# Attention on one Trainium2 core: value products of two steps together, maxima over two adjoining PSUM banks, first group's maxima in the projection stage

## The chip, the cores and the metric

The kernel is one program on one core of a Trainium2 chip. The metric is the device time of one execution in microseconds (us). The engines are called as in the profile: PE (TensorE matmuls), PEld (its weight loads), DVE (VectorE), ACT (ScalarE), POOL (GpSimd), SP (SyncE, which here only issues DMAs). PSUM has eight banks of 512 fp32 columns.

## The reference

One layer of a mixed model, on x of shape 4 x 1024 x 256 (4096 tokens): low-rank multi-head attention, a spiking feed-forward block, a selective scan (Mamba-like), and the feed-forward block again, each with a norm and a residual. The change touches attention only:

```
xn = layernorm(x)                        # per token, 256 channels
q  = latent_q @ Wu_q + rope(latent_q @ Wq_r)
k  = latent_kv @ Wu_k + rope(xn @ Wk_r)
v  = latent_kv @ Wu_v                    # 16 heads of 16 channels
p  = softmax(q @ k.T / sqrt(272))        # 1024 x 1024 per head and batch
x  = x + (p @ v) @ Wo + bo
```

## The kernel before

`program` calls `project`, `attend`, `merge_heads`, `feed_forward`, `scan` and `feed_forward` in turn; each is a block of its own with a program for every engine, joined by semaphores. Engines take their instructions strictly in the order in which they are written.

**project** runs over 8 tiles of 512 tokens (two per batch). PE computes latents, rotary and compact parts in fp32. DVE joins them (`rotate`, `join`); ACT and POOL split each result into three bf16 parts (`high`, `middle`, `lower_parts`); SP stores the parts to the DRAM scratch `qk_parts`, 16 DMAs a tile (L216). `parts` has one buffer, so `high` of a tile waits for the stores of the tile before (`parts_out`). At tile 6 SP also loads the stacks of group 0 with `load_stack` (13 DMAs, L532 and L535).

**attend** works on 16 groups; a group is 4 heads of one batch. The bf16 parts are stacked along the contraction (96 rows), so that one bf16 matmul gives scores of near fp32 accuracy; three more rows carry the negated row maxima, which are subtracted in the same matmul. Three kinds of matmul are interleaved on PE:

- `for_max` (L762): scores with queries on the partitions, for the *next* group. 64 units of 128 x 512, in three PSUM banks by turns (`max_bank`, `MB` = 3). DVE's `maximum` (L864) reduces each to one column. Each `for_max` waits on `reduced` until the unit three before it has been reduced.
- `scores` (L776): scores with keys on the partitions, for the current group, in two pairs a step. Each pair fills a two-bank tile `score_bank[pair]` (4 banks in all), and ACT takes its exp (L852) into `probs`, which has two buffers, one a step.
- `pv` (L819): 4 matmuls of 32 output rows each, one for each head, side by side in the array; fp32, so each makes two passes and the trace shows eight records. They accumulate in `o_bank` (one bank) over 8 steps, one half group. `keep_o` (DVE, L883) then copies it out and SP stores it.

A group has 16 steps, and a step of PE is: scores pair 0, M0, scores pair 1, M1, M2, `pv` of the step before, M3, where M0 to M3 are four `for_max` units. Twice a group `turn` (PE, L769) transposes the row maxima of a half and `negate` (DVE, L877) negates them; POOL splits them in three (`split`) and SP writes them in as stack rows. `groups` runs 15 groups as 5 passes of a hardware loop, three groups a pass; at the end of a pass PE drains (`pv` of step 15). The 16th group comes behind it, without `for_max`.

The maxima of group 0 have no group before them. They stand ahead of the loop in `attend`: PE makes 32 pairs of matmuls into the two score tiles (L831), DVE reduces each pair, 1024 wide, straight into `row_max` (L912).

Of the kernel before, what the change touches and what calls it, by code (L numbers as in the profile page):

```python
# [118 lines left out]
def project(nc, io, xT, vT, split_scr, q_stack, k_stack):  # L119
# [6 lines left out]
    with ExitStack() as ctx:  # L126
        m = Mem(nc, ctx)
        ident = m.sb("ident", [P, P])
# [24 lines left out]
        comp_bank = [m.bank(f"comp_bank{c}") for c in range(DC)]  # L153
        rot_bank = [m.bank(f"rot_bank{c}") for c in range(DC)]
# [10 lines left out]
        stack_in = m.sem("first_stack_in")  # L165
# [15 lines left out]
        OUT = 16 * NG  # L181
        block = ctx.enter_context(nc.Block())
# [6 lines left out]
        def _(sp):  # L189
# [12 lines left out]
            for t in range(NT):  # L202
# [16 lines left out]
            sp.wait_ge(stack_in, STACK_LOAD)  # L219
            for u in range(CHUNKS):  # L220
                sp.wait_ge(parts_out[u], OUT * NT)

        @block.gpsimd
        def _(pool):
            nc.gpsimd.memset(mean_w[:], 1.0 / D).then_inc(consts_set, 1)
            nc.gpsimd.memset(eps_col[:], EPS).then_inc(consts_set, 1)

# [29 lines left out]
            lower_parts(NT - 1, 0)  # L257

        @block.tensor
        def _(pe):  # L260
# [45 lines left out]
            def rotary(t, side):  # L306
                for c in range(DC):
                    cols = slice(c * P, (c + 1) * P)
                    if side == 1:
# [3 lines left out]
                        for k in range(DC):  # L313
                            mm = nc.tensor.matmul(rot_bank[c][:], wkr[:, k, cols], xn[:, t % 2, k],
                                                  start=(k == 0), stop=(k == DC - 1))
                    else:
# [3 lines left out]
                        mm = nc.tensor.matmul(rot_bank[c][:], wq[:, 1, cols], ct[:, 0], start=True, stop=True)  # L320
                    mm.then_inc(proj_ready, 1)

            def compact(t, side):
                for c in range(DC):
# [4 lines left out]
                    mm = nc.tensor.matmul(comp_bank[c][:], wkc[:, cols] if side == 1 else wq[:, 0, cols], ct[:, side],  # L329
# [23 lines left out]
            for t in range(NT):  # L353
# [12 lines left out]
                if t + 2 < NT:  # L366
                    mean(t + 2)

# [70 lines left out]
        def _(dve):  # L439
# [26 lines left out]
            def rotate(t, side):  # L466
# [7 lines left out]
                for c, tables in enumerate(((cos, sin), (sin, cos))):  # L474
                    dve.wait_ge(proj_ready, t * UNITS + (ROT_K if side == 1 else ROT_Q) + c + 1)
                    for i, table in enumerate(tables):
                        nc.vector.scalar_tensor_tensor(r[:, 2 * c + i], rot_bank[c][:], bias[:, c:c + 1], table,
                                                       ALU.add, ALU.mult).then_inc(rotated, 1)

            def join(t, side):  # L480
# [3 lines left out]
                for c in range(DC):  # L484
# [3 lines left out]
                    nc.vector.scalar_tensor_tensor(comp_bank[c][:], comp_bank[c][:], bias[:, c:c + 1], r[:, 3 * c],  # L488
                                                   ALU.add, ALU.add).then_inc(rotated, 1)
                for c in range(DC):  # L490
# [6 lines left out]
                    nc.vector.tensor_tensor(full[:, u], comp_bank[c][:], r[:, 2 - c], ALU.subtract if c == 0 else ALU.add)\  # L497
# [15 lines left out]
            for t in range(NT):  # L513
# [8 lines left out]
                join(t, 0)  # L522

# [48 lines left out]
def attend(nc, io, vT, split_scr, q_stack, k_stack, o_scr, recip_scr, early, done_with):  # L572
# [10 lines left out]
    MB = 3  # L583
    TURN_NOW, TURN_NEXT = 2, 10
    with ExitStack() as ctx:
        m = Mem(nc, ctx)
        qs = [q_stack] + [m.sb(f"qs{i}", [P, 2, G, TW], BF16) for i in (1, 2)]
        ks = [k_stack] + [m.sb(f"ks{i}", [P, G, S], BF16) for i in (1, 2)]
        vg = [m.sb(f"vg{i}", [P, QT, G, 2 * HD]) for i in range(3)]
        ident = m.sb("ident_a", [P, P])  # L590
        probs = m.sb("probs", [P, 2, G, TW])
        mx = m.sb("mx", [P, 2, HU])
        row_max = m.sb("row_max", [P, 2, HU // 2])
        neg_max = m.sb("neg_max", [HU // 2, 2, P])
        neg_rest = m.sb("neg_rest", [HU // 2, 2, P])
        neg_parts = m.sb("neg_parts", [HU // 2, 2, 3, P], BF16)
# [4 lines left out]
        max_bank = [m.bank(f"max_bank{i}") for i in range(MB)]  # L601
# [3 lines left out]
        ident_in, ones_set, v_set = m.sem("ident_in"), m.sem("ones_set"), m.sem("v_set")  # L605
# [30 lines left out]
        def _(sp):  # L636
            sp.sem_clear(done_with)
            for h in range(2):
                sp.sem_inc(max_rows_in[h], 16)
# [48 lines left out]
            sp.dma_start(ident[:], io["ident"]).then_inc(ident_in, 16)  # L688

            sp.sem_inc(stack_in[0], STACK_LOAD)  # L690
            load(1, 1)
            max_rows(0, 0, 0)
# [12 lines left out]
        def _(pool):  # L705
            pool.sem_inc(neg_split, 8)
            for i in range(3):
                nc.gpsimd.memset(ks[i][SROWS:MROWS], 1.0).then_inc(ones_set, 1)

                pool.wait_ge(ones_set, 2 * i + 1)  # L710
                nc.gpsimd.memset(vg[i][:, :, :, HD:], 1.0).then_inc(ones_set, 1)
                pool.wait_ge(ones_set, 2 * i + 2)
# [32 lines left out]
            pool.wait_ge(ones_set, 6)  # L745
            v_of(0, 0)
            split(0, 0)
# [5 lines left out]
        def _(pe):  # L753
            pe.sem_inc(scores_ready, 1)
            pe.sem_inc(pv_done, 3 * STEPS)

            def for_max(g, r, a):
# [4 lines left out]
                nc.tensor.matmul(max_bank[(r + a) % MB][:], qs[r][0:SROWS, half, j, qt * P:(qt + 1) * P],  # L762
# [17 lines left out]
            def body(g, r, it, with_next):  # L780
                for s in range(STEPS):
                    if s % QT == 0:

                        pe.wait_ge(max_rows_in[s // QT], g * 48 + 64)
                    if s == 0 and with_next:
# [21 lines left out]
                if r == 2 or not with_next:  # L807
                    pv(g, r, STEPS - 1)

            def pv(g, r, s):  # L810
                qh, kt = s // QT, s % QT
                if s == 0:
                    pe.wait_ge(v_set, g + 1)
                if kt == 0:
# [3 lines left out]
                for j in range(G):  # L818
                    mm = nc.tensor.matmul(o_bank[32 * j:32 * j + 32, :], vg[r][:, kt, j], probs[:, s % 2, j],  # L819
# [3 lines left out]

            pe.wait_ge(stack_in[0], STACK_LOAD)
# [1275 lines left out]
```

## Time and profile before

| | us |
|---|---|
| median of 3 runs | 2124.3 (2123.36 to 2128.74) |
| the profiled execution | 2120.39 |
| its span, first to last instruction | 2118.6 |
| project | 0 to about 179 |
| attend, maxima of group 0 | about 180 to 220 |
| attend, 15 looped groups | 220.6 to about 930 |
| attend, last group | about 930 to 966 |
| merge, feed-forward, scan, feed-forward | the rest |

Mean granted TensorE clock: 0.954 of full speed. A timeline row gives start and length in us, engine, line, output and inputs, a count of merged instructions, and in brackets how long the engine stood idle before and what ended that. In merged rows the length goes from the first start to the last end; records of neighbouring matmuls overlap, since PE is pipelined.

### The profile page before, as it was taken

To read this page: it belongs to the slowest core of one execution; us is meant where nothing else is said; L and a number is where in the kernel's file an instruction comes from. 1 tells how busy PE (TensorE), PEld (TensorE's weight loads), DVE (VectorE), ACT (ScalarE), POOL (GpSimd) and SP (SyncE) were. 2 spreads that over 40 slices of the span, in tenths; PEclk is the share of its full clock that TensorE was granted. 3 is DMA by queue.
4 is the path that set the end of the run, shared out by engine and by line. 5 is a ranking of instruction groups with operands and counts; after the bars stand their busy time and mean duration, and the time that the engine had idled before them with its cause. 6 is when DMAs were issued, how large, how long until landed. Compare 5 with 4: busy or idle time off the path is not lost. (4 is left out here: it accounts for less than half of the span.)

```text
span 2118.6 us, 25344 instructions
## 1 busy us (share of the span) xinstructions
PE 1935.5 (91%) x6834; PEld 728.5 (34%) x6834; DVE 1673.7 (79%) x2442; ACT 1063.5 (50%) x1400; POOL 754.8 (36%) x518
## 2 busy tenths in 40 slices
PE   8996999999999999998999988788878888799997
PEld 4441232322232323323444433333333333234443
DVE  5887898998998989964565568999999999955554
ACT  3441566666666666672222236576567657422221
POOL 2664000000000000000100028999999999810000
PEclk9996899999999999999999999899999999999999
DMA  3454122231221222213100004444544445300000
GB/s 105 113 120 85 36 41 47 49 61 44 41 46 42 41 47 41 41 51 115 40 0 0 0 15 126 121 116 115 121 112 118 118 117 155 90 0 20 15 15 30
DMA packets 94683, 138.30 MB, mean 65 GB/s; under 512 B 13616, under 2 KB 52800, under 8 KB 93024
## 3 DMA queue, kind: packets, MB, share of 16 engines
q1 hardware_dynamic: 94560, 136.79, 26.8%
q8 instruction: 61, 1.00, 0.2%
q14 instruction: 62, 0.51, 0.1%
HBM read 110.27 MB, written 26.08 MB: 64 GB/s over the span
## 5 line engine op out<-in xcount | busy, mean ns | idle before, releaser
L864 DVE TENSOR_REDUCE mx<-max_bank 128x1 f32<-128x512 f32 x960 | 617.9, 687 | 57.9 <-PE max_bank L762 57.5
L852 ACT ACTIVATE probs<-score_bank 128x1024 f32<-128x1024 f32 x512 | 496.6, 1021 | 295.0 <-PE score_bank L776 294.7
L762 PE MATMUL max_bank<-ks,qs 96*128 96x512 bf16 x960 | 333.4, 388 | 0.0
L776 PE MATMUL score_bank<-qs,ks 99*128 99x512 bf16 x1024 | 310.5, 386 | 15.0 <-issue 13.2
L1538 POOL TENSOR_TENSOR ring<-u,bc 128x1024 f32<-128x1024 f32 x128 | 301.6, 2364 | 10.0 <-ACT u L1734 10.0
L1608 PE MATMUL ys_bank<-outs,rec_diag 128*128 128x512 f32 x512 | 254.1, 627 | 43.5 <-POOL outs L1546 22.0
L819 PE MATMUL o_bank<-probs,vg 128*32 128x512 f32 x2048 | 272.7, 605 | 0.7 <-ACT probs L852 0.7
L1546 POOL TENSOR_TENSOR outs<-ring,bc 128x1024 f32<-128x1024 f32 x109 | 257.7, 2364 | 25.6 <-DVE ring L1941 25.6
L728 POOL CAST neg_parts<-neg_max 16x128 bf16<-16x128 f32 x32 | 9.0, 281 | 682.8 <-DVE neg_max L877 682.8
L1783 ACT ACTIVATE a_bank<-dt,decay_s 128x512 f32<-128x512 f32 x256 | 169.5, 684 | 146.8 <-DVE ring L1941 103.5
L1332 ACT ACTIVATE relu_f<-hid_bank_f 128x512 f32<-128x512 f32 x128 | 76.4, 597 | 327.5 <-PE hid_bank_f L1285 282.4
L1357 DVE SCALAR_TENSOR_TENSOR hid_f<-hid_bank_f,relu_f 128x512 f32<-128x512 f32 x128 | 86.9, 688 | 189.5 <-ACT relu_f L1332 188.5
L1261 PE MATMUL y_bank_f<-hid_f,wpr_f 128*128 128x512 f32 x512 | 234.2, 592 | 0.5 <-DVE hid_f L1357 0.5
L1932 DVE SCALAR_TENSOR_TENSOR ring<-a_bank,ring 128x512 f32<-128x512 f32 x256 | 171.5, 670 | 24.3 <-ACT a_bank L1783 23.9
L762 PEld LDWEIGHTS max_bank<-ks,qs 96*128 96x128 bf16 x960 | 93.7, 98 | 277.9 <-DVE mx L864 184.2
L1608 PEld LDWEIGHTS ys_bank<-outs,rec_diag 128*128 128x128 f32 x512 | 100.9, 201 | 184.7 <-issue 134.8
L982 POOL TENSOR_TENSOR sq_sum_f<-sq_f 128x512 f32<-128x512 f32 x16 | 20.2, 1265 | 390.1 <-ACT sq_f L1009 390.1
L776 PEld LDWEIGHTS score_bank<-qs,ks 99*128 99x128 bf16 x1024 | 99.0, 99 | 121.7 <-issue 25.2
L1261 PEld LDWEIGHTS y_bank_f<-hid_f,wpr_f 128*128 128x128 f32 x512 | 95.9, 190 | 120.7 <-issue 115.8
L1941 DVE TENSOR_TENSOR_SCAN ring<-a_bank,ring 128x512 f32<-128x512 f32 x112 | 135.6, 1211 | 0.0
L1941 DVE TENSOR_TENSOR_SCAN ring<-a_bank,state,ring 128x512 f32<-128x512 f32 x106 | 134.8, 1271 | 0.0
L1285 PE MATMUL hid_bank_f<-xn_f,wfc_f 128*128 (+1 forms) x256 | 119.5, 600 | 3.2 <-POOL eps_col_f L951 3.2
(198 smaller groups left out, 2150.6 us busy)
## 6 DMA issues: line engine op xcount, KB each, us to landing
bc<-bc_scr SPq DMA_DIRECT2D x128, 512.0 KB, 4.9
qk_parts<-parts SPq DMA_DIRECT2D x128, 96.0 KB, 1.9
qs<-qk_parts SPq DMA_DIRECT2D x128, 64.0 KB, 4.3
o_scr<-o_sb SPq DMA_DIRECT2D x32, 256.0 KB, 2.1
ks<-qk_parts SPq DMA_DIRECT2D x16, 384.0 KB, 4.7
xin<-in_x_dram SPq DMA_DIRECT2D x8, 512.0 KB, 3.9
ks<-qk_parts SPq DMA_DIRECT2D x16, 256.0 KB, 3.5
qs<-qk_parts SPq DMA_DIRECT2D x32, 128.0 KB, 4.8
```

The costliest lines, as they stand in the source:

```text
L762: nc.tensor.matmul(max_bank[(r + a) % MB][:], qs[r][0:SROWS, half, j, qt * P:(qt + 1) * P], ks[r][0:SROWS, j, kh * TW:(kh + 1) * TW], star ...
L776: mm = nc.tensor.matmul(score_bank[pair][:, j % 2], ks[r][0:MROWS, j, kt * P:(kt + 1) * P], qs[r][0:MROWS, qh, j, :], start=True, stop=True)
L819: mm = nc.tensor.matmul(o_bank[32 * j:32 * j + 32, :], vg[r][:, kt, j], probs[:, s % 2, j], start=(kt == 0), stop=(kt == QT - 1))
L852: nc.scalar.activation(probs[:, s % 2, 2 * pair:2 * pair + 2], score_bank[pair][:], ACT.Exp, scale=SOFTMAX_SCALE).then_inc(probs_ready, 1)
L864: nc.vector.tensor_reduce(mx[:, a // HU, a % HU:a % HU + 1], max_bank[(r + a) % MB][:], AX_X, ALU.max)\
L1261: mm = nc.tensor.matmul(y_bank[c][:], wpr[:, f, c * P:(c + 1) * P], hid[:, f], start=(f == 0), stop=(f == FC - 1))
L1538: nc.gpsimd.tensor_tensor(ring[:, g % RING], u[:, t % 2], bc[:, g % BC, 0:1].to_broadcast([P, DC, TW]), ALU.mult).then_inc(inputs, 1)
L1546: nc.gpsimd.tensor_tensor(outs[:, g % OUTS], ring[:, g % RING], bc[:, g % BC, 1:2].to_broadcast([P, DC, TW]), ALU.mult).then_inc(weighted, 1)
L1608: mm = nc.tensor.matmul(y_bank[f][:], rec_diag[:, f * NS + n], outs[:, g % OUTS, f], start=(n == 0), stop=(n == NS - 1))
L1783: nc.scalar.activation(a_bank[g % 2][:, f], dt[:, t % 2, f], ACT.Exp, scale=a_col[:, f, n:n + 1])\
L1932: nc.vector.scalar_tensor_tensor(x, a, 1.0, x, ALU.subtract, ALU.mult).then_inc(scaled, 1)
L1941: nc.vector.tensor_tensor_scan(a if on_dve(g) else x, a, x, state[:, f, n:n + 1] if t % TPB else 0.0, ALU.mult, ALU.add)\
```

## The change

Four edits, all in the attention part:

1. **Value products together.** `pv` runs on even steps only and then for the two steps before. `probs` gets four buffers (`KEPT`). `keep_o` goes from DVE to ACT and stands behind the exps of steps 0 and 8.
2. **Maxima over two banks.** The three max banks become one tile `max_banks`. Where a unit lies in bank 0, `maximum` takes it and the next one (bank 1) in one instruction of 2 x 512; units in bank 2 are taken alone. It waits for both matmuls, and raises `reduced` by two when it is done.
3. **First group.** The 32 wide maxima of group 0, the turn, negation, splitting and writing of their first half go to the end of `project`'s programs, in the banks of rotary and compact parts. The stacks of groups 0 and 1 are both loaded by SP at tile 3 (before: group 0 at tile 6, group 1 at the start of `attend`).
4. **Constants.** POOL sets the ones rows of two stacks at the start of `project`, and the other ones behind the first `v_of` in `attend`; PE waits for them at its first `pv` and at step 8. The identity is shared, its second load is gone.

```diff
 def project(...)
+        max_banks = (rot_banks, comp_banks)
 @sync
-                if t == NT - TPB:
+                if t == TPB + 1:
                     for u in range(CHUNKS):
-                        sp.wait_ge(parts_out[u], OUT * t)
-                    load_stack(sp, split_scr, q_stack, k_stack, 0, stack_in)
+                        sp.wait_ge(parts_out[u], OUT * TPB)
+                    for g in range(2):
+                        load_stack(sp, split_scr, begun[f"qs{g}"], begun[f"ks{g}"], g, stack_in)
...
+            sp.wait_ge(neg_split, 4)
+            for part in range(3):
+                sp.dma_start(begun["qs0"][SROWS + part:SROWS + part + 1, 0], neg_parts[:, 0, part, :]).then_inc(neg_in, 16)
 @gpsimd
+            for g in range(2):
+                nc.gpsimd.memset(begun[f"ks{g}"][SROWS:MROWS], 1.0).then_inc(ones_set, 1)
+                pool.wait_ge(ones_set, g + 1)
 @tensor, behind the last tile
+            pe.wait_ge(stack_in, 2 * STACK_LOAD)
+            for n in range(PAIRS):
+                if n == 0:
+                    pe.wait_ge(rotated, (NT - 1) * SIDES * ROTS + ROTS + 4)
+                elif n == 1:
+                    pe.wait_ge(summed, NT * CHUNKS)
+                else:
+                    pe.wait_ge(unit_max, n - 1)
+                for kh in range(2):
+                    mm = nc.tensor.matmul(max_banks[n % 2][:, kh], ...)
+                mm.then_inc(unit_ready, 1)
 @vector, behind the last tile
+            for n in range(PAIRS):
+                dve.wait_ge(unit_ready, n + 1)
+                nc.vector.tensor_reduce(row_max[:, half, i:i + 1], max_banks[n % 2][:].rearrange("p a t -> p (a t)"),
+                                        AX_X, ALU.max).then_inc(unit_max, 1)

 def attend(...)
+    KEPT = 4
-        probs = m.sb("probs", [P, 2, G, TW])
+        probs = m.sb("probs", [P, KEPT, G, TW])
+        max_banks = ctx.enter_context(nc.psum_tensor("max_banks", [P, MB, TW], F32))
+        max_bank = [max_banks[:, i] for i in range(MB)]
 @gpsimd
+            nc.gpsimd.memset(vg[0][:, :, :, HD:], 1.0).then_inc(ones_set, 1)
...
+            v_of(0, 0)
+            for i in (1, 2):
+                nc.gpsimd.memset(vg[i][:, :, :, HD:], 1.0).then_inc(ones_set, 1)
+            nc.gpsimd.memset(ks[2][SROWS:MROWS], 1.0).then_inc(ones_set, 1)
 @tensor
-                    if s > 0:
-                        pv(g, r, s - 1)
-                    elif r > 0:
-                        pv(g - 1, r - 1, STEPS - 1)
+                    if s % 2 == 0:
+                        if s > 0:
+                            pv(g, r, s - 2)
+                            pv(g, r, s - 1)
+                        elif r > 0:
+                            pv(g - 1, r - 1, STEPS - 2)
+                            pv(g - 1, r - 1, STEPS - 1)
 @scalar
-                    act.wait_ge(pv_done, g * STEPS + (3 * STEPS + s - 1))
+                    act.wait_ge(pv_done, g * STEPS + (3 * STEPS + s - KEPT + 1))
...
+                    if s == 0 and r > 0:
+                        keep_o(g - 1, 1)
+                    if s == QT:
+                        keep_o(g, 0)
 @vector
             def maximum(g, r, a):
-                dve.wait_ge(max_ready, g * UNITS + a + 1)
-                nc.vector.tensor_reduce(mx[:, a // HU, a % HU:a % HU + 1], max_bank[(r + a) % MB][:], AX_X, ALU.max)\
-                    .then_inc(reduced, 1)
+                bank = (r + a) % MB
+                if bank == 1 and a:
+                    return
+                n = 2 if bank == 0 and a + 1 < UNITS else 1
+                dve.wait_ge(max_ready, g * UNITS + a + n)
+                nc.vector.tensor_reduce(mx[:, a:a + n], max_banks[:, bank:bank + n], AX_X, ALU.max).then_inc(reduced, n)
-            def keep_o(g, qh):
-                nc.vector.tensor_copy(o_sb[:, qh], o_bank[:]).then_inc(o_kept, 1)
```

## Rows read from the trace of the kernel before

**Rows 1.** The page: busy time, share of the span, instructions.
```profile
PE 1935.5 (91%) x6834; PEld 728.5 (34%) x6834; DVE 1673.7 (79%) x2442; ACT 1063.5 (50%) x1400; POOL 754.8 (36%) x518
```

**Rows 2.** Timeline of PE in the loop: start, length in us, line, tiles, idle before.
```profile
442.65 0.39 PE L762 MATMUL max_bank<-ks,qs 96*128 96x512 bf16 x1
...
443.97 0.60 PE L762 MATMUL max_bank<-ks,qs 96*128 96x512 bf16 x2
444.49 1.07 PE L819 MATMUL o_bank<-probs,vg 128*32 128x512 f32 x8
445.49 0.39 PE L762 MATMUL max_bank<-ks,qs 96*128 96x512 bf16 x1
```

**Rows 3.** The same stretch on DVE, then on ACT.
```profile
443.08 2.59 DVE L864 TENSOR_REDUCE mx<-max_bank 128x1 f32<-128x512 f32 x4 [0.25 <-PE max_bank L762]
...
443.51 1.94 ACT L852 ACTIVATE probs<-score_bank 128x1024 f32<-128x1024 f32 x2 [0.96 <-PE score_bank L776]
```

**Rows 4.** Timeline of DVE: two negations of neighbouring halves.
```profile
299.39 0.28 DVE L877 TENSOR_SCALAR neg_max<-max_bank 16x128 f32<-16x128 f32 x1 [0.23 <-PE max_bank L769]
...
322.31 0.28 DVE L877 TENSOR_SCALAR neg_max<-max_bank 16x128 f32<-16x128 f32 x1 [0.22 <-PE max_bank L769]
```

**Rows 5.** Waits from 250 to 900 us (in total, times, longest); then line 819.
```profile
PEld max_bank L762 <- DVE mx L864: 168.7, 218, 0.8
...
L819 PE MATMUL o_bank<-probs,vg x2048: 589/593/618, 226.4 to 965.1; 128*32 128x512 f32 x187
```

**Rows 6.** Timeline of all engines, first step of a loop pass.
```profile
364.16 4.33 DVE L864 TENSOR_REDUCE mx<-max_bank 128x1 f32<-128x512 f32 x7 [2.86 <-PE max_bank L762]
...
364.91 0.10 PEld L762 LDWEIGHTS max_bank<-ks,qs 96*128 96x128 bf16 x1 [0.41 <-DVE mx L864]
```

**Rows 7.** Groups by line: the wide maxima; then timeline of PE, fp32 matmuls.
```profile
L912 DVE TENSOR_REDUCE row_max<-score_bank 128x1 f32<-128x1024 f32 x32 | 37.7, 1220 | 12.2 <-PE score_bank L831 11.2 <-DVE row_max L912 0.2
...
118.87 1.88 PE L303 MATMUL lat_bank<-xn,wdq 128*128 128x512 f32 x4
```

**Rows 8.** Timeline of the last group.
```profile
958.43 3.90 ACT L852 ACTIVATE probs<-score_bank 128x1024 f32<-128x1024 f32 x4 [0.32 <-PE score_bank L776]
...
964.66 1.07 PE L819 MATMUL o_bank<-probs,vg 128*32 128x512 f32 x8 [0.66 <-ACT probs L852]
```

**Rows 9.** Timeline between projection and the loop.
```profile
155.86 21.31 SPq L216 DMA_DIRECT2D qk_parts<-parts  x32
...
168.68 1.28 DVE L497 TENSOR_TENSOR full<-comp_bank,rot 128x512 f32<-128x512 f32 x2
...
179.98 1.89 PE L831 MATMUL score_bank<-ks,qs 96*128 96x512 bf16 x4 [13.72 <-SPq L690]
...
181.13 19.32 DVE L912 TENSOR_REDUCE row_max<-score_bank 128x1 f32<-128x1024 f32 x16 [11.17 <-PE score_bank L831]
...
220.57 1.03 PE L776 MATMUL score_bank<-qs,ks 99*128 99x512 bf16 x2 [1.89 <-issue]
```

**Rows 10.** Projection: the queue of SP, then ACT.
```profile
98.44 11.04 SPq L216 DMA_DIRECT2D qk_parts<-parts  x16
...
148.03 1.27 SPq L532 DMA_DIRECT2D ks<-qk_parts  x3
149.34 6.48 SPq L535 DMA_DIRECT2D qs<-qk_parts  x10
...
110.58 1.15 ACT L408 ACTIVATE parts<-full 128x512 bf16<-128x512 f32 x2
...
...
117.41 0.67 ACT L400 ACTIVATE ct<-lat_bank,bcol 128x512 f32<-128x512 f32 x1
```

**Rows 11.** Windows: stretch, length, busy time by engine (instructions), granted clock, DMA.
```profile
190.00:205.00 15.00, 12.82 (x27) 1.71 (x25) 14.48 (x13) 0.00 (x0) 2.16 (x3) 0.50 0.01 2
646.00:652.00 6.00, 5.99 (x15) 2.09 (x15) 3.27 (x5) 3.30 (x4) 0.00 (x0) 0.50 0.02 4
950.00:960.00 10.00, 9.75 (x60) 1.81 (x58) 0.10 (x1) 9.29 (x10) 0.39 (x1) 1.00 0.52 160
```

More of the change, by code:

```diff
@@ L152, in project @@
         norm_bank, lat_bank = m.bank("norm_bank"), m.bank("lat_bank")
-        comp_bank = [m.bank(f"comp_bank{c}") for c in range(DC)]
-        rot_bank = [m.bank(f"rot_bank{c}") for c in range(DC)]
+        comp_banks, rot_banks = (ctx.enter_context(nc.psum_tensor(n, [P, DC, TW], F32)) for n in ("comp_banks", "rot_banks"))
+        comp_bank, rot_bank = ([banks[:, c] for c in range(DC)] for banks in (comp_banks, rot_banks))
         ident_in, consts_in = m.sem("ident_in"), m.sem("consts_in")
@@ L600, in attend @@
         recip_parts = m.sb("early_parts", [2 * EARLY, 3, TW], BF16)
-        max_bank = [m.bank(f"max_bank{i}") for i in range(MB)]
+        max_banks = ctx.enter_context(nc.psum_tensor("max_banks", [P, MB, TW], F32))
+        max_bank = [max_banks[:, i] for i in range(MB)]
         score_bank = [m.ctx.enter_context(nc.psum_tensor(f"score_bank{i}", [P, 2, TW], F32)) for i in range(2)]
         o_bank = m.bank("o_bank")
-        ident_in, ones_set, v_set = m.sem("ident_in"), m.sem("ones_set"), m.sem("v_set")
+        ones_set, v_set = m.sem("ones_set"), m.sem("v_set")
         stack_in = [m.sem(f"stack_in{i}") for i in range(3)]
@@ L686, in body @@
                 o_to_dram(g, 1)
[L688 to L692, printed above, removed]
+            for g in range(2):
+                sp.sem_inc(stack_in[g], STACK_LOAD)
             with sp.Fori(0, (NGT - 4) // 3) as it:
@@ L705, in _ @@
         def _(pool):
[L706 to L712, printed above, removed]
+            pool.sem_inc(neg_split, 12)
+            nc.gpsimd.memset(vg[0][:, :, :, HD:], 1.0).then_inc(ones_set, 1)
+            pool.wait_ge(ones_set, 1)
             def v_of(g, r):
@@ L761, in for_max @@
                 pe.wait_ge(reduced, g * UNITS + a + 1)
-                nc.tensor.matmul(max_bank[(r + a) % MB][:], qs[r][0:SROWS, half, j, qt * P:(qt + 1) * P],
+                nc.tensor.matmul(max_bank[(r + a) % MB], qs[r][0:SROWS, half, j, qt * P:(qt + 1) * P],
                                  ks[r][0:SROWS, j, kh * TW:(kh + 1) * TW], start=True, stop=True)\
@@ L813, in pv @@
                     pe.wait_ge(v_set, g + 1)
+                    pe.wait_ge(ones_set, 3)
                 if kt == 0:
@@ L818, in pv @@
                 for j in range(G):
[L819 removed]
+                    mm = nc.tensor.matmul(o_bank[32 * j:32 * j + 32, :], vg[r][:, kt, j], probs[:, s % KEPT, j],
                                           start=(kt == 0), stop=(kt == QT - 1))
                 mm.then_inc(pv_done, 1)
[L824 to L839 removed]
+            pe.wait_ge(ones_set, 1)
             groups(pe, body)
@@ L891, in body @@
                             negate(g + 1, 0, turn_bank(r, s))
-                        if i == 3 and s == 0 and r > 0:
-                            keep_o(g - 1, 1)
-                        if i == 3 and s == QT:
-                            keep_o(g, 0)
                         if with_next:
@@ L904, in body @@
                     both_halves(g + 1, 1)
-                if r == 2 or not with_next:
-                    keep_o(g, 1)
-            for n in range(HU):
-                half, i = n // (HU // 2), n % (HU // 2)
-                dve.wait_ge(max_ready, 2 * n + 2)
-                nc.vector.tensor_reduce(row_max[:, half, i:i + 1], score_bank[n % 2][:].rearrange("p a t -> p (a t)"),
-                                        AX_X, ALU.max).then_inc(reduced, 2)
-                if i == HU // 2 - 1:
-                    dve.wait_ge(reduced, 2 * n + 2 + MB)
-                    nc.vector.sem_inc(row_max_ready, 1)
-                if n == HU // 2 + 3:
-                    negate(0, 0, max_bank[0])
             groups(dve, body)
```

127 lines of the change are left out of this document (79 added, 48 removed).

## The prediction

> **What bounds the kernel now.** I read the page's busy shares first, then the main loop of attend between 250 and 900 us in the waits and the timelines of PE, DVE and ACT, then the two ends of attend. Over the whole span PE is busy for 91% and DVE for 79% [rows 1], but a busy PE is not yet a bound, so the loop itself has to be read. There are 15 groups with a next group (five loop passes of three) and a last one without. A step of such a group is, on PE, score pair, M0, score pair, M1, M2, the value product (PV) of the step before, M3; M0 to M3 are the matmuls of `for_max`. [rows 2] show it in steady state. From 442.65 (M3) to 443.97 (M1) six bf16 matmuls start in 1.32 us, 0.22 each. The second of the two at 443.97 would be through at 444.41; PV starts at 444.49, 0.08 later; its eight records take 1.00 until M3 starts at 445.49. So 8 x 0.22 + 0.08 + 1.00 = 2.84 us, the distance of the two M3: PE has no hole. DVE [rows 3] takes four maxima in 2.59 and then waits 0.25 for the M3 behind PV; ACT waits 0.96 in a step. PE bounds the loop, with DVE only 9% below it. The two negations at 299.39 and 322.31 [rows 4] are a whole half group apart: 22.92 = 8 x 2.84 + 0.20 for the transpose.
>
> The waits say that PE's weight loads stand 168.7 us for DVE's maxima [rows 5]. This is not lost time: loads wait while PV still streams. Where PV is absent it is real. In step 0 of a loop pass [rows 6] the maximum of M0, the first of seven, begins at 364.16 and ends 0.69 later, at 364.85; the load of M3, which needs that bank, starts at 364.91, its matmul 0.01 later. So a freed bank reaches PE after 0.07. The other way, M3 at 442.65 to its maximum at 443.08 is 0.43.
>
> **The change, part by part.**
>
> *Maxima over two adjoining banks.* A 1024 wide maximum lasts 1.220 [rows 7]; back to back 16 take 19.32 [rows 9], spaced (19.32 - 1.22)/15 = 1.21, against 2 x 0.63 for two narrow ones ([rows 3], (2.59 - 0.69)/3). That saves 0.05 of DVE time per pair, on an engine that isn't the bound. The Trainium skill (Perfetto Trace Analysis, Optimizing Scalar/DVE Operations) says grouping helps a saturated engine, since each access to PSUM costs DVE about 125 ns; but where DVE is unsaturated and holds up others, smaller instructions may finish sooner. By its 125 ns some 320 pairs would save 40 us of DVE time, by the rows 16; neither is PE time, and its second half speaks against the edit.
>
> The price is in the waits. `maximum` on bank 0 now waits for two matmuls, and both banks come free together. With three banks, call them b0, b1, b2. The next M on b0 must wait for the whole pair maximum, the one on b1 comes after it in PE's order, and only then can the next pair maximum start. From one pair maximum to the next: 1.22 (it lasts) + 0.07 + gap from M(b0) to M(b1) on PE + 0.43. Gaps: 0.22 where they adjoin, 0.66 with two score matmuls between, and with both PVs between 0.22 + 1.94 = 2.16 (1.94 below). 24 maxima, three double steps, have 8 such cycles, and bank 0 falls once on each of the 8 positions of a double step. The gaps then sum to PE's own time of one double step: 16 x 0.22 + 1.94 = 5.44. So 8 x 1.72 + 5.44 = 19.2. Two cycles are longer, as the two PVs stand between M(b1) and the next M(b0) and PE arrives late: with PVs behind M(b1) 2.16 + 0.66 - 0.43 - 1.29 = 1.10, behind M(b2) 0.22 + 2.16 - 0.43 - 1.29 = 0.66. Sum 20.96, or 6.99 per double step, against 2 x 2.84 = 5.68. That is +1.31, x 8 x 15 = **+157 us**. The maxima on b2 fit between the pairs (1.21 + 0.6 = 1.8, the shortest cycle is 1.94), so DVE isn't full: it waits. The new stall is PE's at `for_max`, with the scores and PVs behind it, and ACT behind them.
>
> *Value products of two steps together.* PE leaves and enters PV half as often. An fp32 pass of 512 columns takes (1.88 - 0.59)/3 = 0.43 [rows 7], 0.59 being one record of PV [rows 5]; a PV makes two passes on each of four column strips side by side, 0.86, so 1.00 + 0.08 holds 0.22 of entering and leaving. No row has two PVs adjoining. Bounds: two together cost 1.08 + 0.86 = 1.94 if this is paid once, 2.16 if it is paid each time. I take 1.94, since all eight records are the same form and the 0.22 stands at changes of form. The other end adds 0.22 x 120 = 26 us to the loop. Steps without PV let PE run into the maxima earlier; that is in the cycles above.
>
> *Four probability buffers.* Needed for the above; ACT's wait for `pv_done` lies two steps further back. No cost.
>
> *keep_o to ACT.* A 0.69 copy leaves DVE. On ACT it waits for the joined PV; it starts 0.1 behind it and takes some 0.6 (estimated from exps twice as wide, 1.0), while the next score pair needs 0.22 + 0.22 + 0.4 = 0.85. It hides in ACT's idle time (0.96 a step [rows 3]); uncovered it would be 32 x 0.6 = 19 us. I take 0.
>
> *Last group.* It has no maxima and is bound by the exp chain [rows 8]: four exps in 3.90 and 0.32 of waiting are two steps, 4.22. After two PVs ACT has run dry: score pair 0.63, two exps of 0.92, next score pair from 2.63, first PV at 3.15, plus 1.94, 5.1. Eight times 0.88: 7.0, less the 0.7 that the last PV waited: **+6 us**.
>
> *First group's maxima in projection.* Now DVE ends its last projection work at 169.96 and idles until 181.13; the 32 wide maxima then run to about 220 and the loop starts at 220.57 [rows 9]. They are DVE-bound, 1.21 each, and stay so. In the new place they begin at 170.0, as the banks come free, and hide the splitting and the stores that attend waited for: -11.2. But the switch of blocks now comes behind them. It costs the 0.9 us that PE needed before (SP's last store was issued by 177.17 and took the page's 1.9 to land, at 179.1; PE started at 179.98), the `ones_set` wait for one memset, 0.6, and perhaps cold loop code: +1.5 (0 to 3.5). On SP, 26 loads move to t = 3, where 13 stood at t = 6. Thirteen took 1.27 + 6.48 us to issue [rows 10], so 15.5 from about 91.7 to 107.3; the 16 stores that started at 98.44 start 8.9 late. `high` of the next tile (110.58) waits for their first eight, landed about 114.8 instead of 106; its second half for the last, landed about 120.2. ACT's latent copy at 117.41 is behind it and the PE tile behind that (118.87): about +2.7 (0 to 5), as PE has other matmuls until then. The loads at t = 6 go, without gain: the tile there was no longer than the rest. Two memsets of 3.5 us on POOL fall before its first work at 18.5. Sum: -11.2 + 1.5 + 2.7 = **-7 us**. The loads of groups 0 and 1 and the negated rows are there long before use; the constants set later (`ones_set` 3 and 4) are needed at step 2 and step 8, after 5 and 25 us, and take about 6 us of POOL.
>
> Total: the profiled execution took 2120.4 (span 2118.6). 2120.4 + 157 + 6 - 7 = 2276. The median of the three runs is 3.9 above the profiled one, so I forecast **2280** as a median.
>
> **Rivals.**
>
> *A, forecast, 0.84:* the coupled cycle sets the loop. Its own range is 2254 (handovers shorter by 0.07 in each of 320 cycles, -22; start part at its best, -4) to 2310 (PV saving nothing, +26; start part at its worst, +4).
>
> *B, faster, 0.06:* the pair never ends last and PE stays the bound. Then a double step is 5.44 + two PV margins, 5.46: 0.22 less, x 120 = -26; with -7 and +6 that is 2093 as a profiled execution, 2097 as a median. It decides at 8x + 5.44 + 1.76 = 17.04, x = 1.23 for maximum plus both handovers; the rows give 1.72. Against it: every term of 1.72 was read singly. For it: DVE loses 0.05 per pair and a copy per half group. The Trainium skill (TensorEngine Tiling (Array Packing), Key Properties) holds that changing the tiling mode drains the engine; the 0.22 of [rows 2] agrees with that.
>
> *C, between, 0.03:* the edges cancel, within 0.3% of 2124 (about what a measurement can tell from no change). It needs cycles of 1.3.
>
> *D, clock, 0.07:* with more holes PE falls to the 1.2 GHz level (granted 0.50) and stays. It stood at 0.50 from 190 to 205 in DVE-bound maxima [rows 11], yet at 1.00 in the last group with holes of 0.2 to 0.7; after the hole at a loop end it was 0.50 for some us of dense work, then full again. In the new loop PE has work for 5.4 of 7.0 us, its holes are under 1 us, and at half clock the work (some 10.5) would be dense again, after which it rose before. If one pass of five stayed low, 24 x (10.5 - 7.0) = 84 more: 2360; all of them, 2700.
>
> **Chances.** Faster 0.06, same 0.03, slower 0.91 (A and D). The range 2245 to 2315 is A's with 5 to 9 us beyond the ends for what isn't listed; B, C and D, 0.16 together, are left out, and some 0.04 of A.
>
> **What would show it.** Right: distances of score steps by pairs near 7.0 us; DVE's waits for `max_bank` near 1.1 us a step instead of 0.25; PE idle for maxima in the middle of steps; wide maxima 1.22; copies of `o_bank` on ACT right behind the second PV; the loop starting near 213.5 us; group distance 56 instead of 45.8. Two adjoining PVs in 1.94 or 2.16 settles that term. Wrong: a double step of 5.5, or a granted clock below 0.9 in the loop; or PE reaching M(b0) late so seldom that a cycle is 6.4.

## The result, and the profile after

The changed kernel takes **2298.8 us** (median of 4 runs, 2296.9 to 2301.9) against 2123.8 (2120.7 to 2128.7, 4 runs) for the kernel before: **1.082 times as long**, 95% interval 1.080 to 1.084. Slower was forecast, with 2280 and a range of 2245 to 2315. The profiled execution has a span of 2300.1 and a mean granted clock of 0.952 (before: 2118.6 and 0.954).

The page of the changed kernel: engine totals, then the granted clock in 40 slices, then three groups by line (idle time and its releaser behind the bar).

```profile
PE 1964.1 (85%) x6834; PEld 748.0 (33%) x6834; DVE 1627.8 (71%) x2095; ACT 1087.7 (47%) x1432; POOL 754.8 (33%) x518
...
PEclk9996999999999999999999999899999999899999
...
L937 DVE TENSOR_REDUCE mx<-max_banks 128x1 f32<-128x512 f32 (+1 forms) x645 | 589.0, 947 | 278.0 <-PE max_banks L826 277.8
L913 ACT ACTIVATE probs<-score_bank 128x1024 f32<-128x1024 f32 x512 | 501.3, 1022 | 393.0 <-PE score_bank L840 390.1
L826 PE MATMUL max_banks<-ks,qs 96*128 96x512 bf16 x960 | 338.9, 391 | 158.2 <-DVE mx L937 146.0
```

All three engines of attention have a lower share than in [rows 1], though PE's work is the same 6834 instructions: they wait for each other. The waits between 250 and 1100 us (in total, times, longest) say for whom:

```profile
ACT probs L913 <- PE score_bank L840: 332.3, 248, 4.3
PEld max_banks L826 <- DVE mx L937: 325.6, 323, 1.7
DVE mx L937 <- PE max_banks L826: 265.7, 336, 4.1
PE max_banks L826 <- DVE mx L937: 139.1, 210, 1.2
...
ACT o_sb L905 <- PE o_bank L890: 51.0, 28, 3.6
```

PE waits for DVE and DVE waits for PE, on the same line of each. In [rows 5] only the loads stood there, covered by PV; now PE's matmuls themselves do, 210 times. The coupled cycle can be seen one wait at a time. PE of the changed kernel (start, length, idle before):

```profile
451.17 0.38 PE L826 MATMUL max_banks<-ks,qs 96*128 96x512 bf16 x1
451.39 0.60 PE L840 MATMUL score_bank<-qs,ks 99*128 99x512 bf16 x2
451.82 0.59 PE L826 MATMUL max_banks<-ks,qs 96*128 96x512 bf16 x2
453.59 0.39 PE L826 MATMUL max_banks<-ks,qs 96*128 96x512 bf16 x1 [1.17 <-DVE mx L937]
453.82 0.60 PE L840 MATMUL score_bank<-qs,ks 99*128 99x512 bf16 x2
454.25 0.38 PE L826 MATMUL max_banks<-ks,qs 96*128 96x512 bf16 x1
```

and DVE beside it:

```profile
452.31 1.82 DVE L937 TENSOR_REDUCE mx<-max_banks 128x2 f32<-128x1024 f32 x2 [0.68 <-PE max_banks L826]
454.74 1.82 DVE L937 TENSOR_REDUCE mx<-max_banks 128x2 f32<-128x1024 f32 x2 [0.61 <-PE max_banks L826]
```

M(b0) stands at 451.17, but the wide maximum begins only at 452.31, behind M(b1) at 451.82. It lasts 1.22 (the row also holds the single maximum behind it) and so holds both banks until 453.53; M(b0) follows at 453.59, M(b1) at 454.25 (two score matmuls between them), and the next wide maximum starts at 454.74: 2.43 us from one to the next. This closed chain of waits, in which each engine waits for the other once a pair, is called the ring below.

### The profile page after: what moved, and what is told of

It reads as the page before. It is cut to its first block and busy times, and to the rows that moved or that the text cites. A ratio compares the mean times of both kernels' runs of the same rounds, so it can differ in the third digit from the quotient of the medians.

```text
span 2300.1 us, 25020 instructions
## 1 busy us (share of the span) xinstructions
PE 1964.1 (85%) x6834; PEld 748.0 (33%) x6834; DVE 1627.8 (71%) x2095; ACT 1087.7 (47%) x1432; POOL 754.8 (33%) x518
## 5 line engine op out<-in xcount | busy, mean ns | idle before, releaser
L937 DVE TENSOR_REDUCE mx<-max_banks 128x1 f32<-128x512 f32 (+1 forms) x645 | 589.0, 947 | 278.0 <-PE max_banks L826 277.8
L826 PE MATMUL max_banks<-ks,qs 96*128 96x512 bf16 x960 | 338.9, 391 | 158.2 <-DVE mx L937 146.0
L1596 POOL TENSOR_TENSOR outs<-ring,bc 128x1024 f32<-128x1024 f32 x109 | 258.1, 2368 | 25.5 <-DVE ring L1991 25.5
L890 PE MATMUL o_bank<-probs,vg 128*32 128x512 f32 x2048 | 259.6, 626 | 0.7 <-ACT probs L913 0.7
L826 PEld LDWEIGHTS max_banks<-ks,qs 96*128 96x128 bf16 x960 | 91.8, 97 | 426.7 <-DVE mx L937 340.7
```

What stands on the lines that cost most here:

```text
L826: nc.tensor.matmul(max_bank[(r + a) % MB], qs[r][0:SROWS, half, j, qt * P:(qt + 1) * P], ks[r][0:SROWS, j, kh * TW:(kh + 1) * TW], start=T ...
L937: nc.vector.tensor_reduce(mx[:, a:a + n], max_banks[:, bank:bank + n], AX_X, ALU.max).then_inc(reduced, n)
L1596: nc.gpsimd.tensor_tensor(outs[:, g % OUTS], ring[:, g % RING], bc[:, g % BC, 1:2].to_broadcast([P, DC, TW]), ALU.mult).then_inc(weighted, 1)
```

## The experiments

Ten kernels ran, in three groups, each beside the kernel before (2125.5, 2127.5 and 2125.9 as its medians). Each is described by its change against the kernel named at its diff. Where two kernels come from different groups, the difference of their medians also holds what the groups differ by (up to 2 us in the kernel before), so the ratios are given beside it. The four constants of edit 4 were never measured apart from edit 3.

| kernel | median us | ratio to before (95%) |
|---|---|---|
| e1_single | 2136.8 | 1.0066 (1.0043 to 1.0088) |
| e2_pair_alone | 2261.9 | 1.0654 (1.0624 to 1.0684) |
| e3_first_alone | 2115.5 | 0.9968 (0.9952 to 0.9985) |
| e4_first_keep | 2115.4 | 0.9959 (0.9945 to 0.9974) |
| e5_wait_both | 2204.7 | 1.0362 (1.0328 to 1.0397) |
| e6_free_both | 2181.9 | 1.0259 (1.0223 to 1.0296) |
| e7_wait_and_free | 2299.4 | 1.0811 (1.0771 to 1.0851) |
| e8_pair_over_products | 2164.1 | 1.0185 (1.0152 to 1.0217) |
| e9_keep_scan_later | 2111.2 | 0.9924 (0.9901 to 0.9947) |
| e10_first_scan_later | 2119.2 | 0.9971 (0.9952 to 0.9989) |

### Which of the edits costs: e1 to e4

**e1_single** is the changed kernel with one-bank maxima in the loop:

```diff
-                if bank == 1 and a:
-                    return
-                n = 2 if bank == 0 and a + 1 < UNITS else 1
-                dve.wait_ge(max_ready, g * UNITS + a + n)
-                nc.vector.tensor_reduce(mx[:, a:a + n], max_banks[:, bank:bank + n], AX_X, ALU.max).then_inc(reduced, n)
+                dve.wait_ge(max_ready, g * UNITS + a + 1)
+                nc.vector.tensor_reduce(mx[:, a:a + 1], max_banks[:, bank:bank + 1], AX_X, ALU.max).then_inc(reduced, 1)
```

> The changed kernel with one edit undone: every maximum takes one bank again, waits for one matmul and frees one bank. All else stays (joined value products, four probability buffers, o_bank copied by ACT, first group in projection). Theory A (the two-bank maximum couples PE and DVE): nearly all of the loss goes. The double step falls from 7.11 us to about 5.85 (5.46 of PE's own work, some 0.3 for banks not yet free and 0.1 for exps, since eight maxima now fall into 3.5 us between two blocks of value products); loop pass 142 us instead of 175, whole 2143 us (2130 to 2160). Rival B (the joined value products or the copy on ACT make the loss, by emptying ACT and DVE for 1.9 us at a time): 2260 or more. Rival C (the joined products save PE time and nothing takes it back): 2095.

Measured 2136.8: 162 of the 175 us are gone with this one edit. Its double step, from PV pair to PV pair on PE:

```profile
616.85 1.92 PE L890 MATMUL o_bank<-probs,vg 128*32 128x512 f32 x16
...
622.70 1.92 PE L890 MATMUL o_bank<-probs,vg 128*32 128x512 f32 x16
```

5.85 us, against 5.68 for two steps before. DVE shows where the 0.17 comes from:

```profile
613.28 4.98 DVE L934 TENSOR_REDUCE mx<-max_banks 128x1 f32<-128x512 f32 x8 [0.87 <-PE max_banks L826]
619.13 3.19 DVE L934 TENSOR_REDUCE mx<-max_banks 128x1 f32<-128x512 f32 x5 [0.87 <-PE max_banks L826]
```

During the PV pair PE supplies no maximum and DVE runs dry for 0.87; the other 4.98 of the 5.85 (613.28 to 619.13) are eight maxima of 0.62. Three banks hold three maxima, 1.9 of DVE's work, while the PV pair alone keeps PE for 1.86 (616.85 to the matmul at 618.71) and the next maximum starts 0.42 behind that matmul. With one PV a step DVE's pause was 0.25 [rows 3] and PE had no hole.

**e2_pair_alone** is the kernel before with only the two-bank maxima:

```diff
-                dve.wait_ge(max_ready, g * UNITS + a + 1)
-                nc.vector.tensor_reduce(mx[:, a // HU, a % HU:a % HU + 1], max_bank[(r + a) % MB][:], AX_X, ALU.max)\
-                    .then_inc(reduced, 1)
+                bank = (r + a) % MB
+                if bank == 1 and a:
+                    return
+                n = 2 if bank == 0 and a + 1 < UNITS else 1
+                dve.wait_ge(max_ready, g * UNITS + a + n)
+                nc.vector.tensor_reduce(mx[:, a:a + n], max_banks[:, bank:bank + n], AX_X, ALU.max).then_inc(reduced, n)
```

> The kernel before with the two-bank maximum alone: value products each step, two probability buffers, o_bank copied by DVE, first group's maxima in attend. Theory A: the coupled cycle stands alone, 8 x 1.78 us plus one double step of PE (5.68) plus what arrives late, about 6.8 us per double step instead of 5.68; loop pass 165 us instead of 138, whole 2258 us (2235 to 2275). Rival B (it is the joined value products): 2115 to 2135.

Measured 2261.9, +136 us on its own. The edit costs by itself, with PV in every step. Its PVs at 601.38 and 611.53 are three steps apart, so two steps take 6.77, where 6.8 was expected.

**e3_first_alone** is the kernel before with only the first group's maxima in `project` and the constants (edits 3 and 4). Against the changed kernel it takes back the maxima as e1 does, gives the copy of `o_bank` back to DVE (the lines at e4), and:

```diff
-    KEPT = 4
+    KEPT = 2
 @tensor
-                    if s % 2 == 0:
-                        if s > 0:
-                            pv(g, r, s - 2)
-                            pv(g, r, s - 1)
+                    if s > 0:
+                        pv(g, r, s - 1)
```

> The kernel before with the first group's maxima in projection and the constants set later, alone. From the trace of the changed kernel, whose loop begins 9.8 us earlier (210.73 against 220.57): 2114 us (2111 to 2117). Rival (what is won at the start is given back behind the loop, where the changed kernel stands 3.4 us behind): 2118.

Measured 2115.5: the first group gains 7 us by the ratio, 10 by the medians.

**e4_first_keep** adds four buffers and the copy on ACT to it; PV stays in every step:

```diff
-    KEPT = 2
+    KEPT = 4
 @scalar
+            def keep_o(g, qh):
...
+                nc.scalar.activation(o_sb[:, qh], o_bank[:], ACT.Copy).then_inc(o_kept, 1)
 @vector
-            def keep_o(g, qh):
...
-                nc.vector.tensor_copy(o_sb[:, qh], o_bank[:]).then_inc(o_kept, 1)
```

> The same as e3_first_alone, and o_bank copied by ACT with four probability buffers; value products still each step. Theory: the copy leaves DVE, whose wait grows by it; PE was the bound, so only the places where DVE was late behind the copy and the negation gain, about 0.2 us a group: 2111 us (2108 to 2115). Rival (ACT's copy delays the exps that the next value product waits for): 2120.

Measured 2115.4, no different from e3: the upper edge of what was expected was just missed, and a gain of a few us didn't show. So e1 minus e4 (both of one group) is what joining the PVs costs when the maxima are narrow: +21.4 us, of which 0.17 x 120 = 20.4 is the double step above. From before to after: about -10 (first group and copy), +21 (PVs joined), +162 (two-bank maxima).

### Waiting or instruction: e5 to e7

Is it the 1024 wide instruction, its late start (it waits for two matmuls) or its late end (two banks free at once)? e5 to e7 keep narrow maxima and put the waits alone on them.

**e5_wait_both**: the maximum of bank 0 waits for the matmul of bank 1 too.

```diff
+                n = 2 if bank == 0 and a + 1 < UNITS else 1
+                dve.wait_ge(max_ready, g * UNITS + a + n)
+                nc.vector.tensor_reduce(mx[:, a:a + 1], max_banks[:, bank:bank + 1], AX_X, ALU.max).then_inc(reduced, 1)
```

> The changed kernel with narrow maxima, but the one on bank 0 waits for the matmuls of both banks as the wide one does; each frees its own bank when it is done. Only the late start is kept. Theory A (the schedule of measured handovers worked out for these rules): loop pass 156 us, whole 2206 us (2190 to 2225), so that the late start alone is some 70 of the 162 us between e1_single and the changed kernel. Rival (the length of the wide instruction is the harm): 2137 as e1_single.

**e6_free_both**: it starts at once, but bank 0 is only given back with bank 1.

```diff
+                first, second = bank == 0 and a + 1 < UNITS and a + 1 != HU, bank == 1 and a > 0 and a != HU
+                dve.wait_ge(max_ready, g * UNITS + a + 1)
+                ins = nc.vector.tensor_reduce(mx[:, a:a + 1], max_banks[:, bank:bank + 1], AX_X, ALU.max)
+                if not first:
+                    ins.then_inc(reduced, 2 if second else 1)
```

> The changed kernel with narrow maxima, each waiting for its own matmul, but bank 0 is freed only together with bank 1, when the second maximum is done. Only the late freeing is kept. Theory A: loop pass 150.6 us, whole 2180 us (2165 to 2200). Rival (length of the instruction): 2137.

**e7_wait_and_free**: e6 with the wait of e5, `g * UNITS + a + (2 if bank == 0 and a + 1 < UNITS else 1)`.

> Both rules of the wide maximum (waits for both matmuls, frees both banks at its end) with two narrow instructions in its place. Theory A: the coupling is all; loop pass within 1 to 2 us of the changed kernel, whole 2290 us (2275 to 2305), more than the sum of the late start and the late freeing alone, since only together do they close the cycle. Rival (length of the instruction): 2137 plus what e5 and e6 show, at most 2250.

All three came out within what was expected. Against e1 the late start costs 68 us, the late freeing 45, both together 163 (by the ratios 63, 41 and 158): more than the sum of the two, as was expected because only both rules close the ring. e7, without one wide instruction in the loop, is at 2299.4 (ratio 1.081) not to be told from the changed kernel (1.082). Its rows, DVE and then PE:

```profile
607.71 1.89 DVE L935 TENSOR_REDUCE mx<-max_banks 128x1 f32<-128x512 f32 x3 [0.61 <-PE max_banks L826]
610.13 1.89 DVE L935 TENSOR_REDUCE mx<-max_banks 128x1 f32<-128x512 f32 x3 [0.54 <-PE max_banks L826]
```

```profile
609.05 0.39 PE L826 MATMUL max_banks<-ks,qs 96*128 96x512 bf16 x1 [1.17 <-DVE mx L935]
...
609.72 0.38 PE L826 MATMUL max_banks<-ks,qs 96*128 96x512 bf16 x1
...
611.48 0.39 PE L826 MATMUL max_banks<-ks,qs 96*128 96x512 bf16 x1 [0.73 <-DVE mx L935]
```

The cycle is 2.42 here, 2.43 in the changed kernel. What the wide instruction saves in length (M(b0) follows 1.34 to 1.35 behind the start of the two narrow ones, 1.28 behind the wide one) it loses at its start (0.41 behind the matmul against 0.49). The two waits are enough for the whole loss.

### Where both PVs stand between the matmuls of a pair: e8

**e8_pair_over_products** keeps the wide maximum only where the two PVs separate its matmuls, an eighth of its places and the ones with the longest gap.

```diff
-                if bank == 1 and a:
+                if bank == 1 and a % 8 == 3:
                     return
-                n = 2 if bank == 0 and a + 1 < UNITS else 1
+                n = 2 if bank == 0 and a % 8 == 2 else 1
```

> The changed kernel with a wide maximum at one of its eight places only: where bank 0 holds the third matmul of an even step and bank 1 the fourth, so that both value products stand between them on PE. 8 of 64 units a group come there a third of the time, so 2 to 3 of 21 wide maxima a group are left. Theory A: each such place costs by its gap, 5 us a loop pass, whole 2162 us (2150 to 2175). Rival (any wide maximum costs alike, an eighth of 162 us): 2157; no cost of a wide maximum beyond the joined products: 2137. The first two can't be told apart by the time alone, their place in the step can: the trace should show DVE idle for over 2 us at such a step and PE reaching the next bank 0 late.

Measured 2164.1, 27 us more than e1 (25 by the ratios) for 40 pairs. A double step with such a pair lasts 6.35 (604.68 to 611.03) against 5.85: 40 x 0.5 = 20 of the 27. DVE waits through the PVs with a full bank before it, then PE is late:

```profile
607.04 3.62 DVE L937 TENSOR_REDUCE mx<-max_banks 128x2 f32<-128x1024 f32 x5 [1.53 <-PE max_banks L826]
```

```profile
608.32 0.99 PE L826 MATMUL max_banks<-ks,qs 96*128 96x512 bf16 x3 [0.30 <-DVE mx L937]
```

The time was as expected, DVE's pause not (1.53; over 2 was expected). An eighth of the pairs costs more than an eighth of the 162 us (20), but, as was said before the run, the time alone doesn't separate a cost by the gap (2162) from an equal cost everywhere (2157).

### What is left behind attention: e9 and e10

From the merge's first matmul to the end the changed kernel takes 1153.0 us, the kernel before 1149.6, in unchanged code. The difference of 3.4 lies at the entry of `scan`, which is 4.3 longer; all the rest is 0.9 shorter. Windows of the kernel before (granted clock third from the end, DMA share and GB/s behind it), then of the changed one:

```profile
1259.00:1263.00 4.00, 2.96 (x4) 0.96 (x4) 3.60 (x10) 1.51 (x2) 0.34 (x5) 0.50 0.00 0
1263.00:1268.00 5.00, 4.26 (x9) 1.54 (x9) 1.04 (x6) 3.10 (x6) 3.99 (x1) 0.97 0.22 48
```

```profile
1437.00:1441.00 4.00, 3.65 (x4) 0.96 (x4) 3.83 (x12) 1.49 (x2) 0.30 (x5) 0.50 0.01 4
1441.00:1445.00 4.00, 2.96 (x5) 1.16 (x4) 0.47 (x3) 1.36 (x3) 3.67 (x1) 0.50 0.11 22
1445.00:1449.50 4.50, 4.50 (x7) 1.60 (x6) 0.00 (x0) 4.04 (x6) 3.36 (x1) 0.50 1.01 173
```

PE comes out of a pause at the granted clock 0.50 (the 1.2 GHz level) in both; before it is at the full level for nearly all of the second window, about 3 us behind the scan's first matmul at 1260.04; in the changed kernel only after 1449.5, about 12 us behind that matmul at 1437.36. From the scan's first memset to POOL's first product it is 1259.63 to 1281.03 = 21.40 us before and 1436.96 to 1462.62 = 25.66 after. All kernels showed one of two values: 21.3 to 21.4 (before, e2, e3) or 25.5 to 25.8 (the changed one, e1, e4 to e8). The long value came in every kernel with ACT's copies, which made these a suspect. **e9_keep_scan_later** is e4 with a delay at the scan's entry, and **e10_first_scan_later**, with 5 for 10, is e3:

```diff
+            for n in range(10):
+                nc.gpsimd.memset(unused[:], 0.0).then_inc(delayed, 1)
+                pool.wait_ge(delayed, n + 1)
```

> The kernel of e4_first_keep, and at the entry of the scan POOL writes ten small memsets, one behind the other, into a tile that nobody reads, before the constant on which the first matmul waits, so that TensorE begins some 1 to 2 us later. In e4 the work from the first feed-forward's last counting to the scan's first input took 30.0 us against 25.7 in the kernel before, and its matmuls started 0.85 apart (granted clock 0.50) for 13 us instead of 5. Theory 'moment': which of the two it is depends only on when the dense work begins, so the later start can end in a shorter stretch at 0.50; then this part takes about 27 to 28, and the whole 2111 to 2114. Rival 'cause in attention' (the four buffers or the ACT copies leave something behind that makes this part longer): the part takes 30 plus the added 1 to 2, and the whole 2116 to 2118. Which side of the moment a start falls on can't be read from one trace, so a time of 2116 to 2118 leaves both open unless e10 moves.

> The kernel of e3_first_alone with five such memsets at the entry of the scan, a delay of some 0.5 to 1 us. Theory 'moment': a later start may turn the short stretch at 0.50 into the long one; then this part takes about 30.5 to 31 and the whole some 5 us more, 2120. Rival: 25.8 plus the delay, the whole 2116. A part of 25.8 plus the delay here together with 30 plus the delay in e9 would speak for the rival.

The delays are these rows, of e9 and of e10:

```profile
1244.78 2.03 POOL L1565 MEMSET unused_s<- 128x64 f32 x10
```

```profile
1254.30 0.99 POOL L1565 MEMSET unused_s<- 128x64 f32 x5
```

Windows of e9, then of e10:

```profile
1250.00:1254.00 4.00, 2.96 (x6) 0.96 (x6) 0.00 (x0) 1.65 (x3) 4.00 (x1) 0.89 0.07 18
1254.00:1258.00 4.00, 4.00 (x6) 1.54 (x5) 0.00 (x0) 3.97 (x7) 1.94 (x1) 0.57 0.76 143
```

```profile
1260.00:1264.00 4.00, 4.00 (x5) 1.46 (x6) 0.00 (x0) 1.48 (x3) 4.00 (x1) 0.50 0.25 74
```

e10, which has no ACT copy, went from 21.4 to 26.1 (1254.06 to 1280.18) for 1 us of delay: the long case doesn't need the copies. e9 stayed at 25.6 (1244.53 to 1270.17) though 2 us were put into it; PE was granted the full level earlier (0.89), then fell again for some us (0.57), a course that no other kernel shows. Both speak for the moment at which PE's work begins and against the copies. It is one profiled execution each, and what decides inside the chip wasn't tried. The whole times decide little: e10 came out at 2119.2 (expected 2120 by this theory, 2116 by the rival), but its ratio to the kernel before, 0.9971, is that of e3, 0.9968, which has no delay. e9, expected at 2111 to 2114 (the rival: 2116 to 2118), is the fastest of all at 2111.2, but its interval reaches e4's, so that e9 beats e4 isn't shown.

e9's profile also shows how much one execution is worth: with the same code up to there, its attention ended 5.2 us earlier than e4's (first matmul of the merge at 954.45 against 959.61), though both stood alike at 301 (a pair of scores at 301.46 and 301.44). The granted clock from 350 to 500 and from 500 to 650 was 0.98 and 0.99 in e9, 0.97 and 0.96 in e4. Terms of 2 to 5 us from single profiles can't be told from that.

## Why the prediction was right, and where it was off

By the profiled executions the span grew by 181.5 us, against 2276 - 2120.4 = 156 forecast. Part by part:

| part | forecast | measured |
|---|---|---|
| `project` to the loop's first score | -7 | 210.73 - 220.57 = -9.8 |
| 15 looped groups | +157 | 891.8 - 709.4 = +182.4 |
| last group, to the merge | +6 | 44.6 - 39.1 = +5.5 |
| behind attention | 0 | +3.4 |

**What bounds the loop** was right: the ring over the pair of banks, not the work of an engine. Starts of PV pairs over three double steps:

```profile
583.00 1.92 PE L890 MATMUL o_bank<-probs,vg 128*32 128x512 f32 x16
590.69 1.92 PE L890 MATMUL o_bank<-probs,vg 128*32 128x512 f32 x16
597.51 1.92 PE L890 MATMUL o_bank<-probs,vg 128*32 128x512 f32 x16
604.32 1.92 PE L890 MATMUL o_bank<-probs,vg 128*32 128x512 f32 x16
```

7.69, 6.82 and 6.81, together 21.32 against 20.96: 7.11 a double step, not 6.99. Even the unevenness belongs to the reasoning, since bank 0 falls on another position in each of the three. e7 makes the cause shown and not only argued, and e2 shows that the edit costs +136 without the joined PVs.

**The term that was mis-sized** is the loop's: +157 for what was +182. The step that was off is "1.22 (it lasts) + 0.07 + gap + 0.43": the 0.43 came from a narrow maximum [rows 3], while a wide one starts 0.49 behind its matmul (451.82 to 452.31), so a cycle is 1.22 + 0.06 + gap + 0.49 = 1.77 + gap: 0.05 x 8 x 40 = 16 us, or 0.40 for every three double steps, where 21.32 - 20.96 = 0.36 was measured. (The forecast's 16 x 0.22 + 1.94 is 5.46 and not 5.44, which is 0.8 us in the loop.) The other 9 come from outside the regular cycle. Part of them is a step that the sum left out: the negation queues on DVE behind a wide maximum, and PE waits for the bank of the transpose.

```profile
458.80 1.22 DVE L937 TENSOR_REDUCE mx<-max_banks 128x2 f32<-128x1024 f32 x1 [2.24 <-PE max_banks L826]
459.94 0.27 DVE L949 TENSOR_SCALAR neg_max<-max_banks 16x128 f32<-16x128 f32 x1
```

```profile
458.20 0.28 PE L833 MATMUL max_banks<-ident,row_max 128*16 128x128 f32 x1
...
460.34 0.39 PE L826 MATMUL max_banks<-ks,qs 96*128 96x512 bf16 x1 [1.21 <-DVE neg_max L949]
```

PE stands so ten times between 250 and 1100 us, 12.1 us in all; before, DVE took a negation up within 0.23 of its transpose [rows 4]. In e7, with two narrow maxima under the same rules, ten such waits come to 6.1 us, so about half of the 12.1 goes with the wide instruction; in e1, without the rules, there are none. Yet e7 as a whole is as slow as the changed kernel, so how the 9 divide stays open, and part of it is within the 5 us by which executions differ.

That the range held owes something to luck. Its upper end stood on value products that save nothing (+26) and a start at its worst (+4); neither came. What filled that room was a handover that is longer for a wide maximum, while the range allowed only for shorter handovers (-22).

**Two PVs adjoining**: 441.83 to 443.69 is 1.86, with 0.08 of entry the 1.94 taken; 2.16 is excluded. The Trainium skill's statement that a change of tiling mode drains the array (TensorEngine Tiling (Array Packing), Key Properties) agrees with the 0.22 saved. What the forecast saw only inside its ring is that this saving is worth less than it costs: with narrow maxima it leaves DVE dry for 0.87 of every double step, and e1 is 21.4 us slower than e4. Rival B had 5.46 for a double step with PE as the bound and lacked this step: in e1, where each bank is freed on its own, the double step is still 5.85, and the kernel is slower than before.

**Wide against narrow.** One wide maximum saves 0.07 of length and loses 0.08 of start, so nothing is left of the 0.05 of DVE time per pair in the ring. The Trainium skill (Perfetto Trace Analysis, Optimizing Scalar/DVE Operations) says both that grouping helps a saturated engine and that smaller instructions may be better where an engine holds up others. The second half was the one that applied: e1 with narrow maxima takes 2136.8 against 2298.8. But e7 (2299.4) shows that breaking up the instruction gains nothing while its waits are kept.

**The copy on ACT** lies in ACT's idle time as argued, 0.60 long and 0.07 behind the end of the second PV at 450.57:

```profile
450.64 0.60 ACT L905 ACTIVATE o_sb<-o_bank 128x512 f32<-128x512 f32 x1 [1.51 <-PE o_bank L890]
```

e4 against e3 shows no cost and no gain of it. **The last group** came out at +5.5 for +6; its two-step period is 5.08 (1128.06 to 1133.14) for 5.1.

**The first group** gained 9.8 for 7. The wide maxima begin as the banks come free, 10.0 us earlier than before [rows 9] (11.2 less 2.7 was forecast), and the switch comes behind them:

```profile
171.11 1.21 DVE L579 TENSOR_REDUCE row_max<-rot_banks 128x1 f32<-128x1024 f32 x1
...
207.87 1.22 DVE L579 TENSOR_REDUCE row_max<-comp_banks 128x1 f32<-128x1024 f32 x1
```

```profile
210.73 1.03 PE L840 MATMUL score_bank<-qs,ks 99*128 99x512 bf16 x2 [2.91 <-POOL vg L769]
```

The last ends at 209.09, 1.64 before the loop. Before, the last ended at 220.00, 0.57 before the loop, so the switch added 1.07, where +1.5 was forecast. From the first start to the last end the 32 maxima took 37.98 against 38.87 before, 0.9 that the forecast didn't have. The row names the memset on POOL as what PE waits for, as foreseen. The 26 loads on SP delayed the projection by less than half of the 2.7 taken: the latent matmul of [rows 7] starts at 119.96 instead of 118.87, and its successor of the next tile at 133.30 instead of 132.11. **Rival D**, the clock, did not come: the granted clock is 0.95 to 1.00 in each 100 us of the loop. Only short stretches stood at 0.50, as before, and one of these, behind attention, goes with the last line of the table.

**A better version.** Leave out the wide maxima and the joined PVs, keep the first group's maxima in `project`: e3 (2115.5), e4 (2115.4) and e9 (2111.2) are faster than both kernels, by 0.3 to 0.8% of the kernel before. The delay of e9 is no advice, since its lead over e4 isn't shown.

## What to carry to other kernels

Before one instruction is made to read two buffers that two engines hand to and fro, count the ring: length of the instruction, both handovers, and the other engine's work between the two fills; it is paid once per pair, and with three buffers nothing is left to hide it. Saving an engine's time is worth nothing if neither engine was waiting for that time, and grouping work on one engine (here the value products) empties the queue of the other for as long as the group lasts. Take each handover from a row of the very form that will stand there, and treat differences of a few us between two profiles as unknown until a run moves them.

## What the runs showed of the hardware

- A maximum over two PSUM banks starts 0.49 us behind the matmul that it waits for, one over a single bank 0.41 to 0.43; PE is released 0.06 to 0.07 behind either.
- Two rules of waiting that cost 68 and 45 us alone cost 163 together (63, 41 and 158 by the ratios; e5, e6, e7).
- Two fp32 value products of four column strips each take 1.86 us back to back, behind 0.08 of entry, and one alone takes 1.00 + 0.08.
- Behind the scan's first matmul PE stayed at the 1.2 GHz level for about 3 us in the kernel before and for about 12 in the changed one, and the scan's entry took 21.4 or 25.7 us. With its start shifted by 1 us, e10 showed the long case where e3 had shown the short one, in one profiled execution each.
